# Attention scores as two half-height products among the maxima, the accumulator's copy one step later, and the rotation read from PSUM

## The reference, cut to what matters

```python
q = split_heads(x @ Wq + bq); k = split_heads(x @ Wk + bk); v = split_heads(x @ Wv + bv)   # 16 heads of 16
q = _rope(q); k = _rope(k)             # x1*cos - x2*sin | x1*sin + x2*cos
probs = softmax(q @ k.T / sqrt(16))    # 4096 x 4096 for each head
out = (probs @ v).reshape(S, 256) @ Wo + bo
```

## Time and profile before

| | |
|---|---|
| Runs of the kernel | 3953.18, 3953.17, 3945.92 us; median 3953.17 |
| Profiled execution, its own time | 3957.6 us |
| Its span, first to last instruction | 3955.0 us |
| Mean granted TensorE clock | 0.953 |
| TensorE busy | 3614.0 us, 91% |
| VectorE busy | 3493.7 us, 88% |
| ScalarE busy | 2576.7 us, 65% |
| GpSimd busy | 624.6 us, 16% |
| First block's swap to last reduction of the rotation's parts | 743.0 to 873.8 us |
| First to last maximum of attention | 912.0 to 3744.1 us |

### The profile page before, as it was taken

One profiled execution on the slowest core, in us unless ns is written; L12 is line 12 of the kernel. 1 busy time (PEld: TensorE's weight loads), 2 busy tenths in 40 slices (PEclk: granted clock), 3 DMA queues, 4 the chain that ended last, 5 costly groups with the idle time before them and its releaser, 6 DMA issues. The chain is left out here.

```text
span 3955.0 us, 68507 instructions
## 1 busy us (share of the span) xinstructions
PE 3614.0 (91%) x18757; PEld 1001.7 (25%) x18784; DVE 3493.7 (88%) x5278; ACT 2576.7 (65%) x4673; POOL 624.6 (16%) x436
## 2 busy tenths in 40 slices
PE   5788888857999999999999999999999999999988
PEld 2122222421222222222222222222222222222234
DVE  5999997777999998999999999999999998999815
ACT  5444443550677777777777777777777777777764
POOL 2789894370000000000000000000000000000020
PEclk9899999975899999999999999999999999999999
DMA  1000000341100101010001101000100100010011
GB/s 58 0 1 1 0 0 0 88 99 17 25 13 18 27 3 27 3 27 3 28 12 19 27 3 27 3 27 3 27 19 12 27 3 27 3 27 3 3 53 43
DMA packets 49365, 79.44 MB, mean 20 GB/s; under 512 B 12400, under 2 KB 39536, under 8 KB 44912
## 3 DMA queue, kind: packets, MB, share of 16 engines
q1 hardware_dynamic: 48496, 73.99, 8.2%
q10 hardware_dynamic: 512, 1.05, 0.2%
HBM read 53.37 MB, written 21.23 MB: 19 GB/s over the span
## 5 line engine op out<-in xcount | busy, mean ns | idle before, releaser
L1285 DVE TENSOR_REDUCE part_max<-max_scores 128x1 f32<-128x512 f32 x4096 | 2629.8, 686 | 202.2 <-PE max_scores L1166 154.2
L1267 ACT ACTIVATE prob<-scores 128x512 f32<-128x512 f32 x4096 | 2108.6, 604 | 700.0 <-PE scores L1202 700.0
L1202 PE MATMUL scores<-q_rows,k_rows 99*128 99x512 bf16 x4096 | 1095.6, 387 | 37.2 <-ACT prob L1267 28.4
L1214 PE MATMUL acc<-prob,v_ones 128*32 128x512 f32 x8192 | 1112.7, 616 | 0.0
L1163 PE MATMUL max_scores<-k_twin,q_twin 64*128 64x512 bf16 x2048 | 817.8, 400 | 72.6 <-DMA k_twin<-qk_parts 54.7
L1166 PE MATMUL max_scores<-k_rows,q_rows 64*128 64x512 bf16 x2048 | 818.3, 400 | 20.6 <-DVE part_max L1285 19.6
L1163 PEld LDWEIGHTS max_scores<-k_twin,q_twin 64*128 64x128 bf16 x2048 | 190.1, 93 | 1371.0 <-DVE part_max L1285 1268.1
L1202 PEld LDWEIGHTS scores<-q_rows,k_rows 99*128 99x128 bf16 x4096 | 321.9, 98 | 575.8 <-ACT prob L1267 308.8
L1139 POOL COPY v_ones<-v_all 128x512 f32 (+1 forms) x16 | 9.7, 612 | 2600.6 <-PE acc L1214 2600.5
L512 ACT ACTIVATE decay<-delta,a_scale 128x1024 f32<-128x1024 f32 (+1 forms) x128 | 143.1, 1118 | 300.2 <-DVE scan_state L559 300.2
L597 POOL TENSOR_TENSOR scan_hc<-scan_state,c_rep 128x1024 f32<-128x1024 f32 x128 | 301.8, 2358 | 0.7 <-issue 0.6
(11 more groups left out here) (119 smaller groups left out, 1393.1 us busy)
## 6 DMA issues: line engine op xcount, KB each, us to landing
qk_parts<-roped_parts SPq DMA_DIRECT2D x64, 192.0 KB, 2.9
q_rows<-qk_parts SPq DMA_DIRECT2D x192, 64.0 KB
k_rows<-qk_parts SPq DMA_DIRECT2D x180, 64.0 KB
q_twin<-qk_parts SPq DMA_DIRECT2D x128, 64.0 KB
x_res<-in_x SPq DMA_DIRECT2D x4, 1024.0 KB, 8.8
rope_trig<-in_trig SPq DMA_DIRECT2D x4, 1024.0 KB, 9.0
att_t<-acc_sb SPq DMA_DIRECT2D x128, 32.0 KB
att_all<-att_t SPq DMA_DIRECT2D x8, 512.0 KB, 7.6
```

The costliest lines, as they stand in the source:

```text
L1202: nc.tensor.matmul(sc[:, n % SB, :], k_rows[0:KM, par, kt * P:(kt + 1) * P], q_rows[0:KM, par, q0:q0 + CH], start=True, stop=True).then_in ...
L1214: last = nc.tensor.matmul(acc[32 * i:32 * i + VW, :], v_ones[:, par, kt, :], prob[:, t % PBUF, i * CH:(i + 1) * CH], start=(kt == 0), stop ...
L1267: nc.scalar.activation(prob[:, t % PBUF, j * CH:(j + 1) * CH], sc[:, n % SB, :], ACT.Exp, scale=SCALE).then_inc(exp_done, 1)
L1285: nc.vector.tensor_reduce(part_max[:, t, c:c + 1], mx[:, unit_bank(h, half, u), :], AXX, ALU.max).then_inc(max_read, 1)
```

## The change

1. **Scores.** Each score product over 99 rows becomes two, over rows 0 to 63 (`score_low`) and rows 64 to 98 (`score_high`), that add up in one PSUM bank. The second waits by semaphore for the first (`second_half`). Blocks 0, 2 and 3 begin with the high rows, block 1 with the low ones. A step's 8 half products stand among its 4 maximum units, and `weigh` follows them all. `LEAD` is 19.
2. **Semaphores.** Maxima count on `even_ready` and `odd_ready`, scores on `s_low` and `s_high`, banks freed on `dve_read`; the waits on them are rewritten on all engines. Code for giving some units to ScalarE and GpSimd is added with empty lists (`ACT_CHUNKS = ()`), so it issues nothing. The bank of a unit, its wait for the unit three before it, and `MB` stay.
3. **Accumulator.** `copy_block` follows the exponentials of the second step of the next half (t = 1, `NKT + 1`).
4. **Rotation.** VectorE makes (block + bias) x sin out of PSUM into `cross` and (block + bias) x cos in place in PSUM; ScalarE swaps the halves of `cross`, SBUF to SBUF; VectorE adds the two to `roped`. GpSimd takes the rest and also `low`; it adds no terms any more. A block's PSUM bank comes free when `roped` is made.

```diff
-LEAD = 20
+LEAD = 19
...
+                def swap(g, n):
+                    act.wait_ge(cross_ready, g + 1)
...
+                    nc.scalar.activation(swapped[0:HP, n], cross[HP:P, n], ACT.Copy)
+                    nc.scalar.activation(swapped[HP:P, n], cross[0:HP, n], ACT.Copy).then_inc(swap_ready, 1)
...
-                        nc.gpsimd.tensor_tensor(roped[:, n], term[:, n, 0], term[:, n, 1],
-                                                ALU.add).then_inc(roped_ready, 1)
...
+                def low(g, n):
+                    pool.wait_ge(mid_ready, g + 1)
+                    nc.gpsimd.tensor_tensor(parts[:, n, 2], rest[:, n], parts[:, n, 1],
...
+                    nc.vector.scalar_tensor_tensor(cross[:, n], qb[:, n], b_qk[:, a, h:h + 1],
+                                                   trig[:, 1, bass.ts(i, CH)], ALU.add, ALU.mult).then_inc(cross_ready, 1)
+                    nc.vector.scalar_tensor_tensor(qb[:, n], qb[:, n], b_qk[:, a, h:h + 1],
+                                                   trig[:, 0, bass.ts(i, CH)], ALU.add, ALU.mult).then_inc(own_ready, 1)
...
+                    nc.vector.tensor_tensor(roped[:, n], qb[:, n], swapped[:, n], ALU.add).then_inc(roped_ready, 1)
...
+                def score_low(h, par, t, j):
...
+                    return nc.tensor.matmul(sc[:, n % SB, :], k_rows[0:LANE, par, kt * P:(kt + 1) * P],
+                                            q_rows[0:LANE, par, q0:q0 + CH], start=(j == 1), stop=(j != 1))
+                def score_high(h, par, t, j):
...
+                    return nc.tensor.matmul(sc[:, n % SB, :], k_rows[LANE:KM, par, kt * P:(kt + 1) * P],
+                                            q_rows[LANE:KM, par, q0:q0 + CH], start=(j != 1), stop=(j == 1))
...
+                def second_half(h, par, t, j):
+                    if j == 1:
+                        pe.wait_ge(half_low, h * STEPS + (t + 1))
+                        score_high(h, par, t, j).then_inc(s_high, 1)
+                    else:
+                        pe.wait_ge(half_high, h * (3 * STEPS) + (3 * t + max(j, 1)))
+                        score_low(h, par, t, j).then_inc(s_low, 1)
...
+                        max_stream(h, half, par, u, last_head)
+                        if more:
+                            first_half(nh, npar, nt, 0)
+                            first_half(nh, npar, nt, 1)
+                        max_stream(h, half, par, u + 1, last_head)
+                        if more:
+                            first_half(nh, npar, nt, 2)
+                            second_half(nh, npar, nt, 0)
+                            first_half(nh, npar, nt, 3)
+                        max_stream(h, half, par, u + 2, last_head)
+                        if more:
+                            second_half(nh, npar, nt, 1)
+                            second_half(nh, npar, nt, 2)
+                            second_half(nh, npar, nt, 3)
+                        max_stream(h, half, par, u + 3, last_head)
                         if t > 0:
                             weigh(h, par, t - 1)
...
-                        if t == 0 and not first:
+                        if t == 1 and not first:
                             copy_block(h - 1, 1)
-                        if t == NKT:
+                        if t == NKT + 1:
                             copy_block(h, 0)
```

More of the change, by code:

```diff
@@ L864, in pair @@
                                 copy_turned(i + 1, 1 - b)
[L866 to L870, removed]
+                            swap(g, n)
                             if later(g):
@@ L1035, in unit_slot, with dves_done, lane_ready, position @@
+        def dves_done(h, half, u):
+            own = sum(not by_act(h, half, v) for v in range(u + 1))
+            if is_first(h, half):
+                return own
+            return 2 * NEXT_DVE * h + (NEXT_DVE * (half - 1) + FIRST_DVE + own + (1 if u >= TURN_AT else 0))
+        def lane_ready(h, half, u):
+            return 2 * (MAXU // 2) * h + (MAXU // 2) * half + u // 2 + 1
+        def position(h, half, u):
+            if is_first(h, half):
                 return u + 1
-            return (2 * h + half) * SLOTS + u + (1 if u >= TURN_AT else 0)
+            return u + (1 if u >= TURN_AT else 0)
@@ L1038, in unit_bank @@
         def unit_bank(h, half, u):
[L1039 to L1045 removed]
+            return position(h, half, u) % MB
         def turned(last):
@@ L1139, in copy_v, with copied_max @@
                     nc.gpsimd.tensor_copy(v_ones[:, par, :, 0:DK], mem.v[:, :, bass.ds(h * DK, DK)]).then_inc(v_ready, 1)
+                def copied_max(h, half, u):
+                    n = acts_done(h, half, u)
+                    slot = sum(by_act(h, half, v) for v in range(u)) % COPIES
+                    col = part_col(h, half, u)
+                    both, rest = max_copy[:, slot, :], CH // 2
+                    pool.wait_ge(act_read, n)
+                    steps = Chain(pool, pool_step, (n - 1) * FOLDS)
+                    while rest > FOLD:
+                        steps.link(nc.gpsimd.tensor_tensor(both[:, 0:rest], both[:, 0:rest], both[:, rest:2 * rest],
+                                                           ALU.max))
+                        rest //= 2
+                    nc.gpsimd.tensor_tensor(part_max[:, u // NC, col:col + FOLD], both[:, 0:FOLD],
+                                            both[:, FOLD:2 * FOLD], ALU.max).then_inc(pool_read, 1)
@@ L1275, in _ @@
                 load_even_blocks(act, 0, 0)
+                for u in range(MAXU):
+                    if by_act(0, 0, u):
+                        copy_max(0, 0, u)
+                for u in range(LEAD):
+                    if by_act(0, 1, u):
+                        copy_max(0, 1, u)
                 heads(act, head)
@@ L1477 @@
     by_halves = lambda w: halves(w).reshape(w.shape)
-    swap = lambda w: halves(w)[..., ::-1, :, :].reshape(w.shape)
     by_state = lambda w: np.tile(w.T, (1, CPT))
```

253 lines of the change are left out of this document (165 added, 88 removed).

## The result

The changed kernel takes 3763.38 us (median; 3760.06 to 3765.91), the kernel before 3949.61 in the runs beside it (3945.92 to 3953.18): a ratio of 0.9528 with an interval of 0.9512 to 0.9545. The profiled execution took 3761.9 us against 3957.6, so 195.7 us went; the forecast's sum was -194.

A forecast was written before the change was run, and what follows sets the result against it. TensorE's order, not VectorE, was taken to set the 2.61 us step. 30 x (-3.5 - 3.0 + 0.5) = -180, +12 and -26 made -194: 3957.6 to 3763.6, about 3760 at the median; own range 3720 to 3835, given range up to 3880.

The forecast's parts named there:

- The step: Attention's loop step: from 2.61 to 2.50 us (floor 2.48, up to 2.57), -3.5 us a half.
- both loops of the forecast: In the step: the PSUM bank shared by first and fourth unit (2.48); TensorE's own waits with register instructions (2.50).
- The copy: Accumulator's copy at a half's start: one step later removes most of the stall, -3.0 us a half (bounds 1.85 and 3.45).
- the gap: At a half's start: ScalarE's copy waits for the old half's last `weigh`, holding the scores; 1.85 us more than a step.
- the low clock: Behind the stall at a half's start: granted clock at half, 1.2 GHz; the next step 1.60 us too long.
- The maxima's split: Where VectorE parts the maxima: the 1.42 us excess stays, +0.5 us a half (bounds 0 and +1).
- The last half: Last half, without units: half products alone lengthen its step from 1.97 to 2.34 us, +12 us (bounds 0 and +20).
- The rotation: Rotation ahead of attention: blocks 3.15 instead of 3.96 us apart, -26 us (bounds 0 and -40).
- The sum: Whole kernel: -180 for 30 halves, +12 for the last half, -26 for the rotation, together -194 us.
- The first: Rival, the step: waits cost more, fourth unit at 1.3, step 2.61 as before, about 3868 us; chance 0.22.
- The second: Rival, row tiles: weights load beside running products only where row groups differ; 4256 us, chance 0.07.
- The third: Rival, half products: 35 rows count as another shape than 64; step over 3.2 us, some 4450 us; chance 0.03.

The follow-up runs named there:

- lead20: The changed kernel with LEAD = 20 instead of 19, so that the maximum units come one unit earlier: 4059.52 us, ratio 1.0276.
- short_after: The changed kernel with VectorE reducing only 256 of a unit's 512 keys (output not the reference's): 3685.99 us, ratio 0.9341.
- swap_last: The changed kernel with the fourth unit issued ahead of block 3's second half product instead of behind it: 3824.24 us, ratio 0.9692.
- short_swap: The changed kernel with reductions over 256 of 512 keys and the fourth unit ahead of block 3's second half: 3659.79 us, ratio 0.9275.
- copy_only: The kernel before with the accumulator's copy one step later and nothing else: 3870.55 us, ratio 0.9797.
- last_full: The changed kernel with full score products over 99 rows in the last half: 3748.38 us, ratio 0.949.
- rot_only: The kernel before with the rotation's part of the change alone: 3921.41 us, ratio 0.993.

## Why the prediction was right

**The step.** Forecast 2.50 as 1.18 + 0.32 + 1.00; measured 2.497 in the median, with the fourth unit at 1.19. TensorE's wait for its own product, for which no row of before stood, was taken as 0.45. In this step it is 0.48 from the start of block 0's first half to that of its second, whose tile was busy until 0.45; where the tile was free it is 0.44 (the last half, 3604.53 to 3604.97, and `lead20`, 2400.00 to 2400.44). Block 3's second half comes at 1.14, 0.01 behind the 1.08 to 1.13 of the forecast. `short_after` and `swap_last` show that both loops of the forecast exist, one at 2.49 and one at 2.50; that they tie is chance. By the forecast's count two changes of shape take 0.20 off a step; 0.11 of it reached the time, and the rest went to these two loops (with both of them shorter, in the first head of `short_swap`, the step is 2.44). Per half -3.5 was forecast, and 31 x (2.497 - 2.610) = -3.5 measured.

**The copy.** Forecast -3.0 a half. In the kernel before, the two steps at the change of halves have medians of 4.47 and 3.73, 2.98 more than two of 2.61; in the changed kernel that excess is zero. So the -3.0 was right in size as a share of this change. Alone it is a little less (2.7 by the copies), undone it is more (3.5). The way to it was in part luck. The forecast read one change of halves, with 1.85 for the gap and 1.60 for the low clock, and took a little off. The gap is there at every change, but the step behind it is of two kinds. At 21 of the 31 changes the eight products of the first `weigh` are drawn out as at 2517.96, and the step lasts 4.07 in the median. At the other 10 it lasts 2.61 (`weigh`s at 2158.16, 2162.63 and 2165.24, with a granted clock of 1.00 from 2163 to 2166). With the late copy 2 such slow steps are left in `copy_only` and 1 in the changed kernel; with the copy put back they are 27. So the low clock did go with the gap, but the same gap brings it at some changes and not at others, which no term of the sum had, and that is a part of why one edit is worth 2.7 in one kernel and 3.5 in another.

**The maxima's split.** Forecast +0.5 a half, measured +0.24: the excess is 1.66, from 1.42. Of the typical half the three make -3.5 - 3.0 + 0.2 = -6.3, and its medians are 88.15 and 81.80.

**A gain that the forecast did not see given back.** By the typical half the 30 halves would give 190 us, by the copies (-5.83 a half) they give 175. The rest lies where the loop over heads jumps back to its start, at six of its seven ends. TensorE stands there. The changed kernel, its first product behind one such end, and the loop's own line in TensorE's queue (x count: ns min/median/max; first and last start):

```profile
1474.08 0.60 PE L1263 MATMUL max_scores<-k_rows,q_rows 64*128 64x512 bf16 x1 [3.83 <-issue]
```

```profile
L1123 PEldq COMPARE_BRANCH  x7: 83/3922/4877, 1469.0 to 3468.5; - x7
```

The branch at 1469.0 lasts 4.88 us, the six that jump back between 3.3 and 4.9, and the seventh, which ends the loop, 0.08. Behind the stall the granted clock is at half once more (0.50 from 1474 to 1477), and the products last 0.60 instead of 0.39. A half with such an end takes 5.3 to 6.6 us more than its neighbours in the changed kernel, and 3.5 to 7 more in the kernel before, where it often overlapped with the gap at the half's start; mean halves are 1.22 and 0.83 us above the typical one. Over 30 halves that is about 12 us. It was no term of the sum; against it stands the split, 8 us better than forecast. What the branch waits for was not tried; no kernel here runs without the loop.

**The last half.** Forecast a step of 2.34 and +12; measured 2.41 (2.54 and 2.27 in turn) and +14, and `last_full` gets 15 back. The forecast counted TensorE's own waits alone. In the longer of the two steps the exponentials seem to come in: ScalarE's four of the step before run from 3600.64 to 3602.71, and the first halves of blocks 2 and 3 start at 3602.28 and 3602.76, 0.29 and 0.77 into the step, where 0.22 and 0.50 is what the shorter step shows.

**The rotation.** Forecast a pitch of 3.15 and -26; measured 3.19, and the first `weigh` 24.8 us earlier in the profiled executions, 27 in `rot_only`. The write back to PSUM, taken as 0.75, is 0.75. GpSimd's 1.15 to 1.3 is 1.16, and VectorE's 0.68 to 1.75 is gone.

**The sum.** Attention from first to last `weigh` went from 2808.8 to 2640.0 us, -168.8; the forecast has -180 + 12 = -168. With the rotation -193.6, and the profiled executions differ by 195.7. So the prediction was right by its own mechanism, with errors of its terms (the split on one side, the ends of the loop and the last half on the other) that nearly cancel.

**The rivals.** The first, that the waits eat the step, asked for a fourth unit at 1.3; it comes at 1.19. It is nearer the truth than that looks: `lead20` is this kernel with the same waits in another order, and its fourth unit comes at 1.53 in the median (1.62 in the step shown, 2399.77 to 2401.39). The second, that a tile's weights are not loaded behind its own running product, is refuted. The weight load of the second unit in the step above, in the changed kernel:

```profile
1862.93 0.10 PEld L1260 LDWEIGHTS max_scores<-k_twin,q_twin 64*128 64x128 bf16 x1
```

The unit's weights go to the high rows at 1862.93, while the high half product of 1862.92 streams through the same rows, and the unit itself starts at 1863.15, 0.23 after it. The Trainium skill (TensorE: Matmul & The Clock Gate, part 3) has it that a load overlaps products in flight only where its row group differs; the rows here do not bear that out. They fit its other sentence there, that a load may also be pulled ahead into a background weight buffer. The third, that 35 rows are another shape than 64, is refuted by the same 0.22 between neighbours of both kinds.

## What to carry to other kernels

Products of one array mode cost nothing between each other, whatever their number of rows: here two changes of shape of 0.1 us each went from every step, and 0.11 of them reached the time. The order in which the products are issued can cost more than that: the same products one place off took 0.33 us more a step, 0.18 of it with the last two products that wait on one tile instead of two, the rest through register instructions. Find every loop that could set a step and price each (bank, own wait, register instructions): here two tied, so shortening the bank's alone brought nothing in the loop over heads. Where a step has nothing to be interleaved with, as in the last half, leave the plain products.

## What the runs showed that was not expected

- **The price of a wait on a register's value.** Register instructions of TensorE's queue in the step above, changed kernel, the line of the low second halves' waits (x count: ns; first and last start):

```profile
L1328 PEldq ALU_OP  x3: 32/32/32, 1862.9 to 1863.8; - x3
```

  Each lasts 0.03 us, but kernels whose waits are for constants (the first head) and for registers (the loop) differ by 0.06 us a step (`short_after`: 2.44 and 2.50), 0.08 (`swap_last`: 2.49 and 2.57) and 0.16 (`lead20`: 2.67 and 2.83). No run changes the kind of wait alone, so that the difference is theirs is argued from the two stretches of one kernel.
- **A product that overtakes another.** In `lead20` the low half of 2399.78 (block 1) is issued after the high half of 2400.00 (block 0) and starts before it, while the high rows are busy. In the first head another one does (1102.59, issued behind the high one of 1102.81); in the loop that one starts with it (2400.95 and 2400.96). The Trainium skill (TensorE: Matmul & The Clock Gate, part 3) says that products start strictly in the order of the program; these rows show two that did not.
- **ScalarE reads SBUF a little slower than PSUM**: the swap's copies of 64x512 take 0.628 us from SBUF and 0.594 from PSUM.
- **VectorE and GpSimd.** With one operand of each VectorE operation in PSUM, GpSimd's 128x512 subtraction went from a median of 1.60 to 1.16 us. The Trainium skill (SBUF — State Buffer, on its two separate sides) says that a VectorE operation with both inputs in SBUF and a GpSimd operation that reads SBUF exclude each other; these rows agree, for before the change VectorE's last difference had both there.
